# A two-layer graph network: step order of the first layer, transfers of the second

## The reference, cut to what matters

```python
# layer 0: mean of the neighbours, one dense layer
mean = segment_sum(x[src], dst, N) / maximum(deg, 1)[:, None]
h    = concatenate([x, where(deg > 0, mean, x)], -1)
x    = layernorm(x + relu(h @ W.T + b))
# layer 1: typed attention over the edges
Q, K, V = (type_matmul(x, W_, node_type) for W_ in (W_Q, W_K, W_V))     # 4 node types
k_t     = type_matmul(K[src], W_edge, edge_type)                        # 8 edge types
scores  = sum(Q[dst] * k_t, -1) / sqrt(128) * mu[edge_type]
attn    = sparse_softmax(scores, dst, N)
x       = layernorm(x + segment_sum(V[src] * attn[:, None], dst, N))
```

## Time and profile before

| | us |
|---|---|
| median of 3 runs | 3579.48 (3570.99 to 3601.28) |
| profiled execution | 3594.51, span 3592.7 |
| PE busy | 2618.7 (73%) |
| DVE, ACT busy | 1554.8 (43%), 1151.8 (32%) |
| POOL busy | 2244.9 (62%) |
| mean granted TensorE clock | 0.839 of 2.4 GHz |

### The profile page before, as it was taken

The page is one execution under the profiler, slowest core; times in us unless marked ns, Lnnn a source line. Parts: engine busy times, 40 slices in busy tenths (PEclk is TensorE's granted clock), DMA queues, the critical chain, the costliest instruction groups (busy, mean ns, idle before and its releaser), DMA issues.

```text
span 3592.7 us, 38408 instructions
## 1 busy us (share of the span) xinstructions
PE 2618.7 (73%) x13802; PEld 1868.6 (52%) x13802; DVE 1554.8 (43%) x4730; ACT 1151.8 (32%) x2057; POOL 2244.9 (62%) x2302
## 2 busy tenths in 40 slices
PE   3587888887878827777777777777777777777777
PEld 1355566555556625555554555555555555555555
DVE  8476677666667613322322233322322333323223
ACT  4344454444444412222222222222222222222222
POOL 7665566566556454666666666666666666666664
PEclk9799999899999968777778887777777877777778
DMA  6244354444444432333333333333333333333332
GB/s 157 62 129 121 111 144 130 120 126 120 119 119 126 118 122 75 100 99 100 100 100 101 103 100 100 99 97 100 100 100 102 102 100 101 100 99 100 101 100 69
DMA packets 256960, 384.03 MB, mean 107 GB/s; under 512 B 100640, under 2 KB 189003, under 8 KB 250625
## 3 DMA queue, kind: packets, MB, share of 16 engines
q0 software_dynamic: 108112, 273.13, 27.6%
q1 hardware_dynamic: 146833, 107.53, 9.7%
q10 hardware_dynamic: 1824, 0.92, 0.1%
HBM read 304.30 MB, written 77.13 MB: 106 GB/s over the span
## 4 chain that ended last, share of the span: by engine, by line
POOL 36%; PE 25%; issue 18%; another core or an unknown queue 13%; DVE 5%; ACT 2%; DMA 0%; ACTq 0%; DVEq 0%; POOLq 0%
POOL ring L722 35%; PE banks L777 9%; PE banks L769 4%; PE banks L803 3%; PE banks L850 1%; PE banks L862 1%; PE banks L992 1%; PE banks L855 1%; PE banks L1005 1%; ACT picks L1138 1%; PE banks L1029 1%; PE banks L865 1%; PE banks L1021 1%; POOL ring L717 1%
## 5 line engine op out<-in xcount | busy, mean ns | idle before, releaser
L722 POOL DMA_INDIRECT ring<-kv_table,src_n x1563 | 1485.4, 950 | 798.3 <-issue 447.6
L1005 PE MATMUL banks<-identf,ring 128*128 128x128 f32 x1568 | 436.9, 373 | 630.4 <-issue 501.1
L717 POOL DMA_INDIRECT ring<-x_part_rows,work x462 | 475.1, 1028 | 307.4 <-PE banks L803 142.8
L1005 PEld LDWEIGHTS banks<-identf,ring 128*128 128x128 f32 x1568 | 250.9, 182 | 791.1 <-issue 585.2
L777 PE MATMUL banks<-sums,picks 128*126 128x385 bf16 x2401 | 608.1, 342 | 33.3 <-ACT picks L1138 15.3
L1138 ACT ACTIVATE picks<-banks 128x343 bf16<-128x343 f32 x882 | 433.3, 512 | 543.7 <-PE banks L769 333.6
L1227 ACT ACTIVATE work<-banks 128x512 f32<-128x512 f32 x392 | 213.5, 598 | 887.6 <-remote 638.9
L1623 DVE SCALAR_TENSOR_TENSOR sums<-sums,corr,banks 128x128 f32<-128x128 f32 x98 | 34.0, 347 | 1029.2 <-remote 1022.6
L1219 ACT ACTIVATE work<-banks,negmax 128x2048 f32<-128x2048 f32 x98 | 192.8, 1968 | 807.9 <-issue 743.7
L777 PEld LDWEIGHTS banks<-sums,picks 128*126 128x126 bf16 x2401 | 331.6, 143 | 149.4 <-issue 54.1
L769 PE MATMUL banks<-sums 128*128 128x343 bf16 x882 | 286.1, 325 | 168.7 <-issue 105.8
(11 more groups left out here) (260 smaller groups left out, 2363.3 us busy)
## 6 DMA issues: line engine op xcount, KB each, us to landing
kv_table<-ring SPq DMA_DIRECT2D x48, 1024.0 KB
ring<-kv_table,src_n POOLq DMA_INDIRECT x1563
sums<-x_typed SPq DMA_DIRECT2D x99, 128.0 KB
x_typed<-work SPq DMA_DIRECT2D x49, 256.0 KB
ring<-x_part_rows,work POOLq DMA_INDIRECT x462
x_part_rows<-sums SPq DMA_DIRECT2D x7, 675.5 KB, 7.1
src_n<-x_part_rows,work POOLq DMA_INDIRECT x224
sums<-x_rows SPq DMA_DIRECT2D x51, 64.0 KB
```

What stands on the lines that cost most here:

```text
L717: pool.indirect_dma_start(near[k % RUNS][:, j, :], None, part_dram, bass.IndirectOffsetOnAxis(ap=col_ids[:, first + j:first + j + 1], axis ...
L722: pool.indirect_dma_start(kv_ring[u][:, j, :], None, table, bass.IndirectOffsetOnAxis(ap=of, axis=0)).then_inc(l1_rows[2 * u + j // RUN], 16)
L1005: tr = pe.transpose(bank[KEY_BANK[g]][:, j * P:(j + 1) * P], kv_ring[k.u][:, g * 4 + j, 0:D], identf[:, :])
```

## The change

- POOL no longer computes in the first layer: `weights` moves to DVE at step 0, `edge_keys` becomes four fused instructions on DVE in steps 1 and 2. The third gather buffer moves from `src_n` to `spare_n`.
- DVE's step has another order: `normalise_x1` stands behind `join_parts` of the next step, `belong(i + 1, 0)` behind all `hot` batches, the one-time work in the middle. `belong` is seven compares in bf16 instead of one in f32. The digit operations are cut into thirds, 27 of them in steps 4 to 30, stored at tile 30.
- The picks stand at other slots, `wait_hot` of the next step moves to slot 2, and four of ACT's copies come one pick later.
- SP loads eight windows, four blocks of `moves`, and four groups of x1 rows at a time, and stores four groups of output rows at a time. Their buffers lie in `picks`. The row of ones comes from DRAM (`one_row`, filled once).

```diff
+    WINS, MOVES, ROWS = 8, 4, 4
+    Y_GROUPS = PAIRS1 // ROWS
-        iota_g = sb("iota_g", [P, P])
+        iota_g = sb("iota_g", [P, P], BF16)
-        near_runs = [..., src_n[:, 0:HALF * TW // 2].bitcast(F32)]
+        near_runs = [..., spare_n[:, 0:HALF * TW // 2].bitcast(F32)]
-        x1_rows = [later_part(D) for _ in range(2)]
-        y_rows = [later_part(D) for _ in range(2)]
-        typed_rows = [by_window(later_part(NT * WIN)) for _ in range(2)]
+        group_part = parts(picks, [0], TILES * P)
+        x1_rows = [by_type(group_part(ROWS * D)) for _ in range(2)]
+        y_rows = [by_type(group_part(ROWS * D)) for _ in range(2)]
+        typed_rows = [group_part(NT * WINS * WIN).rearrange("p (t w) -> p t w", t=NT) for _ in range(2)]
...
-                if t == 12:
-                    sp.wait_ge(digit_vec, DIGIT_OPS)
+                if t == 30:
+                    sp.wait_ge(digit_vec, DIGIT_ALL)
...
             sp.wait_ge(l1_init, 1)
             for k in range(2):
+                sp.dma_start(moves[k][0:1, :], ones_dram.rearrange("(a e) -> a e", a=1)).then_inc(moves_loaded[k], 16)
                 load_typed(k)
-                load_moves(k, k, moves_loaded[k])
-                load_rows(k, k, x1_loaded[k])
+                load_moves(k)
+                load_rows(k)
...
-            sp.wait_ge(queries_ps, 1)
-            load_typed(2)
             for b in range(NBLK):
                 sp.wait_ge(score_ps, b + 1)
-                if b + 3 <= NBLK:
-                    load_typed(b + 3)
-                if b + 2 < NBLK:
-                    load_moves(b + 2, b % 2, moves_loaded[b % 2])
-                if b % 2 == 1 and b >= 3:
-                    i = (b - 3) // 2
-                    store_y(i)
...
+                if b % WINS == WINS - 2 and (b + 2 + WINS) * WIN < (NBLK + 1) * WIN:
+                    load_typed((b + 2) // WINS + 1)
+                if b % MOVES == MOVES - 1 and b + 1 + MOVES < NBLK:
+                    load_moves((b + 1) // MOVES + 1)
...
+                if b % (2 * ROWS) == 1 and b > 1:
+                    g = (b - 2 * ROWS - 1) // (2 * ROWS)
+                    store_group(g)
+                    if (g + 2) * ROWS < PAIRS1:
+                        load_rows(g + 2)
...
             for k in range(2 * ND):
-                if k == RUNS - 1:
-                    edge_keys()
-                    pool.wait_ge(keys_nat, 1)
-                if k == RUNS:
-                    weights()
...
-            PICK_AT = [-(-c * TILES // GCOLS) for c in range(GCOLS)]
+            PICK_AT = [3, 4, 7, 10, 14, 17, 18, 19, 22, 24, 25, 28, 29, 31, 33, 37, 42, 44]
...
-                    if i + 2 < ND and h == TILES - 1:
-                        wait_hot(i + 2, 0)
+                    if 0 < i < ND - 1 and h == 2:
+                        wait_hot(i + 1, 0)
...
-                dve.tensor_tensor(belongs[h], col_keys[:, 1, first:first + HALF].unsqueeze(2).broadcast_to([P, HALF, P]),
-                                  iota_g[:, :].unsqueeze(1).broadcast_to([P, HALF, P]), ALU.is_equal).then_inc(belongs_ready, 1)
+                for j in range(HALF):
+                    ins = dve.tensor_scalar(belongs[h][:, j, :], iota_g[:, :], col_keys[:, 1, first + j:first + j + 1], None,
+                                            ALU.is_equal)
+                ins.then_inc(belongs_ready, 1)
...
             def l0(i, late, early):
-                if DIGIT_STEP <= i < DIGIT_STEP + DIGIT_OPS:
-                    digit_op(i - DIGIT_STEP)
                 if i > 0:
                     join_parts(i - 1, (i - 1) % 2)
+                if late:
+                    normalise_x1(late)
                 if i + 1 < ND:
                     hot(i + 1, (i + 1) % 2, 2)
-                    belong(i + 1, 0)
                 if i > 0:
                     add_nodes(i - 1)
                 if late:
                     by_types(late)
+                if i + 1 < ND:
+                    hot(i + 1, (i + 1) % 2, 3)
                 if early:
                     mean(early, added(i))
                 if i + 1 < ND:
-                    for q in range(3, BATCHES):
+                    for q in range(4, BATCHES):
                         hot(i + 1, (i + 1) % 2, q)
+                    belong(i + 1, 0)
+                if i == 0:
+                    weights()
+                if 1 <= i <= KEY_OPS // 2:
+                    for k in range(2 * i - 2, 2 * i):
+                        edge_keys(k)
+                if DIGIT_STEP <= i < DIGIT_STEP + DIGIT_ALL:
+                    digit_op(i - DIGIT_STEP)
                 if late:
                     copy_low(late)
...
-                if early:
+                if i == ND - 1:
                     normalise_x1(early)
...
-            for k in range(2):
-                dve.memset(moves[k][0:1, :], 1.0)
```

More of the change, by code:

```diff
@@ L178, in gnn_kernel @@
         key_idx = src_n[:, :].bitcast(U32)
-        spare_f = spare_n[:, :].bitcast(F32)
-        spare_b = spare_n[:, :].bitcast(BF16)[:, 0:NAT]
+        half_b = src_n[:, :].bitcast(BF16)[:, 0:NAT]
         def parts(tile, at, end):
@@ L420, in far_sweep @@
                 end(i)
-        CONSTS = 13
+        CONSTS = 14
         key_j = check_a.bitcast(I32)[:, 0:KEY_W]
@@ L429, in gnn_kernel @@
         DIGIT_OPS = 9
+        DIGIT_COLS = [k * CBLKS // 3 * P for k in range(4)]
+        DIGIT_ALL = 3 * DIGIT_OPS
         DIGIT_STEP = 4
+        Y_STORES = [1 + -(-Y_GROUPS // 2) + (PAIRS1 - Y_GROUPS * ROWS) * (1 - Y_GROUPS % 2),
+                    Y_GROUPS // 2 + (PAIRS1 - Y_GROUPS * ROWS) * (Y_GROUPS % 2)]
+        KEY_OPS = 4
+        KEY_COLS = [k * NAT // KEY_OPS for k in range(KEY_OPS + 1)]
         def tile(t):
@@ L689, in _ @@
                                         ).then_inc(gen_loaded, 16)
-            def weights():
-                pool.wait_ge(L["small"], 16)
-                pool.wait_ge(L["weights"], 80)
-                for e in range(ET):
-                    pool.tensor_scalar(we_s[:, e, :], we_s[:, e, :], mu_b[:, e:e + 1], SCALE, ALU.mult, ALU.mult
-                                       ).then_inc(weights_ready, 1)
-            def edge_keys():
-                pool.wait_ge(L["etype"], 48)
-                pool.tensor_scalar(spare_n[:, :], src_n[:, :], float(ET), None, ALU.mult).then_inc(pool_step, 1)
-                pool.wait_ge(pool_step, 2)
-                pool.tensor_tensor(et_n[:, :], spare_n[:, :], et_n[:, :], ALU.add).then_inc(pool_step, 1)
-                pool.wait_ge(pool_step, 3)
-                pool.tensor_copy(key_f, et_n[:, :]).then_inc(keys_nat, 1)
             pool.wait_ge(parts_stored, 16 * (TILES // 7))
@@ L977, in mask @@
             def mask(k):
-                pe.wait_ge(moves_loaded[k.par], 16 * (k.b // 2 + 1))
+                m, at = k.b // MOVES, k.b % MOVES * BLOCK
+                pe.wait_ge(moves_loaded[m % 2], 16 * (m // 2 + 2))
                 for q in range(4):
-                    pe.matmul(bank[q], places[:, :], moves[k.par][0:4, q * 512:(q + 1) * 512], start=True, stop=False,
+                    pe.matmul(bank[q], places[:, :], moves[m % 2][0:4, at + q * 512:at + (q + 1) * 512], start=True, stop=False,
                               skip_group_check=True)
@@ L1638, in y_link, with x1_of, finish @@
                 dve.wait_ge(y_vec, n * 5 + k)
-            def finish(n, kept, k, loaded, value):
+            def x1_of(i):
+                return x1_rows[i // ROWS % 2][:, i % ROWS, :]
+            def finish(n, kept):
                 dve.wait_ge(rows_ready, kept)
@@ L1725, in _ @@
                 if pair is not None:
-                    if pair == 2:
-                        dve.wait_ge(first_stored, 16)
-                    finish_rows(pair, pair % 2, y_stored[pair % 2] if pair > 1 else None, 16 * (pair // 2))
+                    finish_rows(pair)
             pair = PAIRS1 - 1
             keep_rows(0, NBLK)
-            finish(pair, NBLK + 1, pair % 2, x1_loaded[pair % 2], 16 * (pair // 2 + 1))
-            finish_rows(pair, pair % 2, y_stored[pair % 2], 16 * (pair // 2))
+            finish(pair, NBLK + 1)
+            finish_rows(pair)
 _INS = ["x", "src", "dst", "edge_type_8", "node_type_4", "L0_gnn_W", "L0_gnn_b", "L1_gnn_W_Q", "L1_gnn_W_K",
```

128 lines of the change are left out of this document (81 added, 47 removed).

## The result

| | kernel before | changed kernel |
|---|---|---|
| median of 10 runs each | 3578.31 us (3551.95 to 3610.67) | 3604.49 us (3588.03 to 3610.95) |
| profiled execution, span | 3592.7 | 3596.8 |
| ratio | | 1.0074, 95% interval 1.0039 to 1.0109 |

The change makes the kernel 0.7% slower, 26 us by the medians. The forecast was 65 us faster.

The account below looks back on a forecast made before the run. Bound: in the first layer POOL's double bursts, in the second POOL's stop and TensorE's late signals holding each other up. Sum: -15 - 50 + 0 + 0 = -65, so 3579.5 - 65 = 3515 us; range 3395 to 3625.

Parts of the forecast that it names:

- Part 1: Start of the first layer: `edge_keys` and `weights` leave POOL, -15 us; bounds 0 and -28 us.
- Part 2: First layer's steps: DVE's new order, bf16 `belong` and later picks reduce double bursts, -50 us; bounds -140 and +126.
- I assume 11: -50 us: First layer: 11 steps with double bursts assumed after the change, about 17 of 48 before; -50 us.
- double bursts: First-layer steps, about 17 of 48, where POOL runs on into the next burst without pausing; each about 8 us longer.
- The 20 us of longer gathers: First layer: 14 more bf16 compares a step lengthen gathers, 0.4 us a step; taken as 0, +20 us as bound.
- Part 3: Second layer: fewer, larger SP transfers are not on the path; 0 us, the block stays 23.1 us.
- Rival C: Second layer: fewer packets let `values`' signal through, 3215 or 3400 us (chance 0.09), or POOL runs on, 3905 (0.05).
- A: Whole kernel: nothing that counts moves, double bursts keep their number, start gives 0 to 15 us; 3565 to 3595, chance 0.22.
- B: First layer: POOL runs on more often, more double bursts; 3690 us at two steps of three, 3623 at half; chance 0.14.

Follow-up runs that it names:

- after_again: The changed kernel itself, unchanged, run again on another chip (chip 0) as a control: 3703.6 us, ratio 1.0222 to the kernel before.
- bf16_delay: Kernel before with bf16 `belong` and a 512-column POOL iota (0.5 us) ahead of each half step's seven gathers: 3786.6 us, ratio 1.0445.
- pause_l1: Changed kernel with a 1024-column POOL iota after the fourth of seven gathers of each first-layer half step: 3570.9 us, ratio 0.9845.
- pause_twice: Changed kernel with a 1024-column POOL iota behind the second and fifth gather of each first-layer half step, on chip 2: 3134.4 us, ratio 1.0402.

## Why the prediction was wrong

**Part 1, the start: right.** -15 was taken, -17.2 measured at the third step, which starts at 127.0, before the 135 that was named. The first `run_sum` comes at 81.2 instead of 74.0; since it comes at 74.6 in after_again, the same program, this is no effect of the change that is shown. It is inside the 17.2. In after_again the third step starts at 133.0, still before 135.

**Part 2, the step that failed.** Its words were "`belong` becomes seven bf16 compares" with "as before" for their time, and "I assume 11: -50 us". In place of the -50 the stretch from the third step to the last `run_sum` took 27.5 us more. The price of `belong` was taken from DVE's time, 1.1 us for 1.09 (seven take 1.23), and nothing else. But alone this edit costs 3.6%, some 130 us, and it has an effect on another engine: it took away 62 hold-ups of POOL's gathers (about 0.6 us each, 40 us of POOL's time). That the second makes the first is not shown; bf16_delay speaks against it. The sum's other mistake is the one that hid this: it took 21.2 us as the length that a step has once double bursts are gone. That length was measured where POOL is late: in the regular steps from 1138 to 1212 us its buffer had been free for 1.7 to 3.9 us when it took it. With POOL a buffer ahead there is no double burst either, but a step is 24 to 27 us. And a sum of single prices could not show that the edits of this loop belong together, one that breaks the good steps and others that repair most of it.

**The 20 us of longer gathers: the wrong sign.** I drew them from the number of bf16 compares and quoted the Trainium skill on the two-port mode (SBUF — State Buffer, "SBUF: two separate sides"). With 14 more such compares a step, gathers became 51 ns shorter (977 for 1028 ns). The rows that could have said so were in the earlier trace rows: a gather of 1.68 us beside a two-input compare of 1.09. The measurement decides, and for the gathers it is the two-input compare. A price of the bf16 compares shows elsewhere: against the iotas of pause_l1 it is DVE that waits.

**Part 3: right in time, and nothing speaks against its reason.** Block 23.05 for 23.10, a POOL wait of 3.17 us in the block shown, 1.0001 alone. Rival C, that larger packets let the signal through, did not come true in either form.

**The rivals.** A, the class that came true (within 1%), gave 3565 to 3595 and argued that nothing moves. Much moved, and it cancelled: that the time came out near it is luck. B expected more double bursts; there are none. That POOL gains lead is right, but its buffer is then not free in time more often: what follows is a wait behind every burst and not running on. The time 3604 lies inside the range, the sign was wrong.

**What stays open.** Why a signal of TensorE that the trace has ready arrives late while POOL issues gathers, and why it does so on four chips and not on the fifth. Slower transfers do not show: in the changed kernel the last packet behind a block's last gather ends 2.4 us after that gather's start, and on chip 2 the profile has a gather of this layer land 2.8 us after its issue. And how the bf16 compares lengthen the steps, where a delay of 0.5 us a half step does not stand in for the lost hold-ups. Shown are the edit that does it, the idle time of TensorE and the lower clock that come with it (5.8 for 4.1 us a step, 0.90 for 0.94), and that an iota within each burst, which holds up DVE too, takes the idle time from 5.9 to 3.6 us.

## What to carry to other kernels

Price an edit on every engine that shares something with the instruction, not on its own engine alone: a form that costs one engine as much as before can change when another one runs. And a pause made of an instruction is not only a pause: look at what it does to the other engines. Take the length of a good step as the length of a state, and ask who is ahead in it, before counting on it for all steps. Where two edits of a diff touch the same loop, run each alone: here one cost 3.6%, and on the same chip the rest of the first layer's part hid four fifths of that.

## What was not expected of the hardware

The same program takes 3013 us on one chip and 3583 to 3637 on four others. The granted clock is not enough to explain it: in the stretch from 300 to 900 us it was 0.95 for pause_twice there and 0.95 for pause_l1 elsewhere, and in the second layer, where it was 0.84 there and 0.78 to 0.80 elsewhere, a block on chip 2 takes the 20 us of POOL's 16 gathers. The difference is plain in one place, the time from the recorded end of `values` to DVE's start: 0.04 us on the one, 9.6 us (2411.9 to 2421.5) on another. And a change can be 0.7% slower in one measurement and 2.2% on another chip.

Two engines hold each other up in both directions: a gather of 0.95 us takes 1.68 beside an f32 compare with two inputs, and seven bf16 compares of 1.23 us take 2.45 beside an iota of 1.00.
